# A Mamba and FFN block on one core: decays from a PSUM tile into a four-slot SBUF ring, and single-row loads of the B and C rows

## The reference

```python
def _L0_attn_ref(x, W_xproj, W_dt, b_dt, A_log, Dp):
    xz = jnp.einsum('btd,pd->btp', x, W_xproj)
    dt_raw = xz[..., :dt_rank]                     # dt_rank 64, d_s 16
    Bm = xz[..., dt_rank:dt_rank + d_s]
    Cm = xz[..., dt_rank + d_s:]
    dt = jax.nn.softplus(jnp.einsum('btr,dr->btd', dt_raw, W_dt) + b_dt)
    A = -jnp.exp(A_log)
    dA = jnp.exp(dt[..., None] * A)
    dBx = dt[..., None] * Bm[:, :, None, :] * x[..., None]
    def step(h, inp):
        dA_t, dBx_t, C_t = inp
        h = dA_t * h + dBx_t
        y = jnp.einsum('bds,bs->bd', h, C_t)
        return (h, y)
    ...
    return ys.transpose(1, 0, 2) + Dp * x

x = L0_attn_x                                      # (16, 1024, 256) float32
x = _layernorm(x + _L0_attn_ref(x, ...), axis=-1)
x = _layernorm(x + _L0_ffn_ref(x, w_gate, w_up, w_down), axis=-1)   # silu(gate) * up, hidden 768
```

## Time and profile before

| What | Before |
|---|---|
| Median of 3 runs | 2022.29 us (2020.32 to 2025.22) |
| The profiled execution's own time | 2022.87 us |
| Its span, first to last instruction | 2021.1 us |
| DVE busy | 1869.1 us, 92% of the span |
| POOL busy | 1768.4 us, 87% |
| PE busy | 1729.2 us, 86% |
| ACT busy | 1474.9 us, 73% |
| TensorE's mean granted clock | 0.947 |
| Transfers' share of 16 DMA engines | 33.3% |

### The profile page before, as it was taken

The page is one execution under the profiler, slowest core; times in us unless marked ns, Lnnn a source line. Parts: engine busy times, 40 slices in busy tenths (PEclk is TensorE's granted clock), DMA queues, the critical chain, the costliest instruction groups (busy, mean ns, idle before and its releaser), DMA issues.

```text
span 2021.1 us, 35597 instructions
## 1 busy us (share of the span) xinstructions
PE 1729.2 (86%) x10664; PEld 1339.9 (66%) x10664; DVE 1869.1 (92%) x2317; ACT 1474.9 (73%) x2668; POOL 1768.4 (87%) x811
## 2 busy tenths in 40 slices
PE   5688888888889888889888889888889888889887
PEld 3566676666677666777666776666766666766665
DVE  5899999999999999999999999999999999999993
ACT  6767777777777778777677877777777778776752
POOL 5998889988988988988988899989889989889970
PEclk7899999999999999999999999999999999999989
DMA  7234333233333233333234233234233243232300
GB/s 248 95 98 137 104 119 116 86 123 135 105 117 115 83 126 131 105 105 125 89 126 130 96 110 120 100 126 131 95 110 113 96 136 121 99 115 88 112 12 21
DMA packets 102675, 223.18 MB, mean 110 GB/s; under 512 B 9617, under 2 KB 44018, under 8 KB 102642
## 3 DMA queue, kind: packets, MB, share of 16 engines
q1 hardware_dynamic: 102642, 222.78, 33.3%
HBM read 203.87 MB, written 18.87 MB: 110 GB/s over the span
## 4 chain that ended last, share of the span: by engine, by line
PE 49%; issue 15%; ACT 14%; DVE 13%; POOL 7%; DVEq 1%; ACTq 0%; POOLq 0%; DMA 0%; SPq 0%
PE p_o L997 16%; PE p_y L960 13%; PE p_m L984 6%; POOL h L416 5%; DVE h L707 4%; DVE hid L743 3%; DVE h L699 3%; ACT p_da L533 3%; PE p_m L908 3%; PE p_c L937 3%; PE p_m L900 3%; ACT da_k L533 2%; ACT res_n L576 2%; PE p_da L928 2%; DVE silu_g L737 2%
## 5 line engine op out<-in xcount | busy, mean ns | idle before, releaser
L406 POOL TENSOR_TENSOR ub<-u,b_bc 128x1024 f32<-128x1024 f32 x384 | 906.1, 2375 | 0.1
L416 POOL TENSOR_TENSOR h<-h,c_bc 128x1024 f32<-128x1024 f32 x320 | 757.0, 2378 | 0.0
L533 ACT ACTIVATE p_da<-dt,neg_a 128x512 f32<-128x512 f32 x768 | 524.1, 686 | 231.2 <-DVE h L699 229.2
L960 PE MATMUL p_y<-ident,h 128*128 128x128 f32 x4096 | 566.2, 290 | 36.9 <-POOL h L416 36.7
L960 PEld LDWEIGHTS p_y<-ident,h 128*128 128x128 f32 x4096 | 509.7, 150 | 87.0 <-POOL h L416 52.0
L699 DVE TENSOR_TENSOR_SCAN h<-p_da,h_carry,ub 128x512 f32<-128x512 f32 x384 | 474.5, 1266 | 9.2 <-ACT p_da L533 8.3
L699 DVE TENSOR_TENSOR_SCAN h<-p_da,ub 128x512 f32<-128x512 f32 x384 | 452.4, 1208 | 15.0 <-ACT p_da L533 9.3
L997 PE MATMUL p_o<-wt_down,hid 128*128 128x256 f32 x1536 | 352.3, 379 | 3.0 <-DVE res L750 1.6
L997 PEld LDWEIGHTS p_o<-wt_down,hid 128*128 128x128 f32 x1536 | 284.4, 190 | 52.2 <-issue 14.7
L984 PE MATMUL p_m<-x_t,wt_up 128*128 128x512 f16 x744 | 194.3, 384 | 81.1 <-DVE hid L743 81.1
L707 DVE TENSOR_TENSOR h<-h,p_c 128x1024 f32<-128x1024 f32 x192 | 229.9, 1197 | 25.3 <-PE p_c L937 25.3
(11 more groups left out here) (101 smaller groups left out, 1875.7 us busy)
## 6 DMA issues: line engine op xcount, KB each, us to landing
b_bc<-bc_rows_dram SPq DMA_DIRECT2D x128, 768.0 KB, 4.0
c_bc<-bc_rows_dram SPq DMA_DIRECT2D x320, 256.0 KB, 4.2
x_in<-in_L_attn_x SPq DMA_DIRECT2D x32, 512.0 KB, 3.5
out_x<-res_n SPq DMA_DIRECT2D x32, 512.0 KB, 3.0
bc_rows_dram<-bc_rows SPq DMA_DIRECT2D x32, 64.0 KB, 1.6
hid<-in_L_ffn_w_gate SPq DMA_DIRECT2D x1, 768.0 KB, 4.9
hid<-in_L_ffn_w_up SPq DMA_DIRECT2D x1, 768.0 KB, 6.8
res<-in_L_ffn_w_down SPq DMA_DIRECT2D x1, 384.0 KB, 7.2
```

The source lines that it names most:

```text
L406: nc.gpsimd.tensor_tensor(ub[:, i % UB_SLOTS, :, :], u[:, par, :, :], b_bc[:, i:i + 1, :].broadcast_to([P, DH, T]), ALU.mult).then_inc(s_u ...
L416: nc.gpsimd.tensor_tensor(h[:, s % H_SLOTS, :, :], h[:, s % H_SLOTS, :, :], c_bc[:, i:i + 1, :].broadcast_to([P, DH, T]), ALU.mult).then_i ...
L533: nc.scalar.activation(da, dt[:, par, q, :], ACT.Exp, scale=neg_a[:, q, s:s + 1]).then_inc(s_da, 1)
L960: ins = nc.tensor.matmul(p_y_tok[:, k, q * P:(q + 1) * P], h[:, s % H_SLOTS, q, k * P:(k + 1) * P], ident[:, :], start=False, stop=(s == S ...
```

## The change

Four things change.

1. All decays go to one ring `da` in SBUF with four slots. ACT makes them three states ahead (`DA_AHEAD` 3), where it made them one ahead. `da_k` goes. The PSUM tile, renamed `p_ub`, holds the transposed inputs of the K states and nothing else, and PE fills it earlier.
2. The K states are 8, 11, 13 and 14 in place of 3, 7, 11 and 15, and their ACT product is made three states ahead in place of two. The ten states that POOL multiplies by C are 0, 1, 3, 4, 5, 6, 7, 11, 13, 14. `UB_AHEAD` falls from 4 to 3.
3. `b_bc` and `c_bc` become rings of six and five slots. Each row has a load of its own, so a chunk has 12 loads of B and ten of C in place of four and ten. The bytes stay the same.
4. The table `AT` has other numbers.

```diff
-POOL_STATES = (0, 1, 2, 3, 4, 7, 8, 9, 10, 11)
+POOL_STATES = (0, 1, 3, 4, 5, 6, 7, 11, 13, 14)
-UB_AHEAD = 4
-DA_AHEAD = 1
+UB_AHEAD = 3
+DA_AHEAD = 3
+DA_SLOTS = 4
-    "dt_of": (7, 1), "u_of": (7, 1),
+    "dt_of": (7, 0), "u_of": (10, 0),
-K_STATES = (3, 7, 11, 15)
-K_AHEAD = 2
+K_STATES = (8, 11, 13, 14)
+K_AHEAD = 3
-        da_k = sb("da_k", [P, K_SLOTS, DH, T], F32)
+        da = sb("da", [P, DA_SLOTS, DH, T], F32)
-        b_bc = sb("b_bc", [P, NB, T], F32)
-        c_bc = sb("c_bc", [P, NP, T], F32)
+        b_bc = sb("b_bc", [P, B_SLOTS, T], F32)
+        c_bc = sb("c_bc", [P, C_SLOTS, T], F32)
-        p_da = ps("p_da", [P, DH, T])
+        p_ub = ps("p_ub", [P, DH, T])
...
             def broadcast_b(c, j, par):
+                if j >= B_SLOTS:
+                    sp.wait_ge(s_ub, NB * c + (j - B_SLOTS + 1))
+                elif not (isinstance(c, int) and c == 0):
+                    wait(sp, s_ub, NB * (c - 1) + (j - B_SLOTS + NB + 1))
+                s = B_STATES[j]
+                sp.dma_start(b_bc[:, j % B_SLOTS:j % B_SLOTS + 1, :], bc_dram[par:par + 1, s:s + 1, :].broadcast_to(
+                    [P, 1, T])).then_inc(s_b[j % B_SLOTS], 16)
...
             def decay(c, s, par, q):
                 act.wait_ge(s_dt, c + 1)
-                if s in K_STATES:
...
-                    da = da_k[:, i % K_SLOTS, q, :]
-                else:
-                    wait(act, s_scan, 2 * units(c, s) - 2 + q - 1)
-                    da = p_da[:, q, :]
-                nc.scalar.activation(da, dt[:, par, q, :], ACT.Exp, scale=neg_a[:, q, s:s + 1]).then_inc(s_da, 1)
+                wait(act, s_scan, 2 * (units(c, s) - DA_SLOTS) - 1 + q)
+                nc.scalar.activation(da[:, s % DA_SLOTS, q, :], dt[:, par, q, :], ACT.Exp,
+                                     scale=neg_a[:, q, s:s + 1]).then_inc(s_da, 1)
...
                 if s in K_STATES:
                     wait(dve, s_ub_ps, DH * (k_units(c, s) - 1) + q + 1)
-                    da, dbx = da_k[:, K_STATES.index(s) % K_SLOTS, q, :], p_da[:, q, :]
+                    dbx = p_ub[:, q, :]
                 else:
                     i = B_STATES.index(s)
                     if q == 0:
                         dve.wait_ge(s_ub, NB * c + (i + 1))
-                    da, dbx = p_da[:, q, :], ub[:, i % UB_SLOTS, q, :]
+                    dbx = ub[:, i % UB_SLOTS, q, :]
...
-                nc.vector.tensor_tensor_scan(h[:, s % H_SLOTS, q, :], da, dbx, initial, ALU.mult, ALU.add).then_inc(s_scan, 1)
+                nc.vector.tensor_tensor_scan(h[:, s % H_SLOTS, q, :], da[:, s % DA_SLOTS, q, :], dbx, initial,
+                                             ALU.mult, ALU.add).then_inc(s_scan, 1)
...
             def ub_transposed(c, s, q):
                 i = K_STATES.index(s)
                 pe.wait_ge(s_ubt, TT * k_units(c, s))
-                wait(pe, s_scan, 2 * units(c, s) - 2 + q - 1)
+                if i > 0:
+                    wait(pe, s_scan, 2 * units(c, K_STATES[i - 1]) - 1 + q)
+                else:
+                    wait(pe, s_scan, 2 * units(c - 1, K_STATES[-1]) - 1 + q)
```

More of the change, by code:

```diff
@@ L35 @@
     "weights": (7, 1),
-    "x_transposed": (2, 1), "x_out": (2, 1), "project": (3, 0), "rank_out": (4, 1), "bc_out": (4, 1),
-    "project_dt": (4, 1), "softplus_abs": (5, 1), "softplus_exp": (6, 0), "softplus_log": (6, 1),
-    "dt_of": (7, 1), "u_of": (7, 1),
[3 rows of a table removed]
-    "gate_up": (9, 1), "tanh": (9, 0), "silu": (10, 0), "hidden": (10, 1),
[3 rows of a table removed]
-    "bc_turned": (7, 1), "bc_cols": (9, 1),
-}
-K_STATES = (3, 7, 11, 15)
-K_AHEAD = 2
+    "x_transposed": (0, 2), "x_out": (3, 0), "project": (3, 0), "rank_out": (4, 1), "bc_out": (4, 1),
+    "project_dt": (4, 0), "softplus_abs": (5, 1), "softplus_exp": (5, 1), "softplus_log": (6, 0),
+    "dt_of": (7, 0), "u_of": (10, 0),
[3 rows of a table added]
+    "gate_up": (9, 0), "tanh": (9, 0), "silu": (10, 0), "hidden": (10, 1),
[3 rows of a table added]
+    "bc_turned": (8, 0), "bc_cols": (11, 1),
+}
+K_STATES = (8, 11, 13, 14)
+K_AHEAD = 3
 K_SLOTS = 2
-GROUP = 4
 UB_SLOTS = 6
+B_SLOTS = 6
+C_SLOTS = 5
 H_SLOTS = 8
@@ L75, in mamba_ffn_block @@
     NB = N - NK
-    B_GROUP = NB // NK
-    assert K_STATES == tuple(range(GROUP - 1, N, GROUP)) and B_GROUP == GROUP - 1
-    assert NB % UB_SLOTS == N % H_SLOTS == NK % K_SLOTS == 0
+    assert NB % UB_SLOTS == N % H_SLOTS == NK % K_SLOTS == N % DA_SLOTS == 0
+    assert NB == 2 * B_SLOTS and NP == 2 * C_SLOTS and K_STATES[0] > 0
     sum_at = {s: s + SUM_LAG[s in POOL_STATES] for s in range(N)}
     SUM_ORDER = sorted(range(N), key=lambda s: (sum_at[s], s))
-    assert all(sum_at[s] < N or s not in POOL_STATES for s in range(N))
+    assert N - 1 not in POOL_STATES
     x_chunks = x.rearrange("b (h k p) d -> (b h) p k d", p=P, k=TT)
@@ L162, in mamba_ffn_block @@
         p_m = ps("p_m", [P, 2, T])
-        tail_ps = (p_m, p_da)
+        tail_ps = (p_m, p_ub)
         tail_t = (tanh_g[:, :], ub[:, 0, 0, :])
@@ L199, in mamba_ffn_block @@
         s_rows_dram = sem("s_rows_dram")
-        s_b = [sem(f"s_b{k}") for k in range(N // GROUP)]
+        s_rows_kept = sem("s_rows_kept")
+        s_b = [sem(f"s_b{j}") for j in range(B_SLOTS)]
         s_ut_ps = sem("s_ut_ps")
@@ L209, in mamba_ffn_block @@
         s_c_ps = sem("s_c_ps")
-        s_c = [sem(f"s_c{i}") for i in range(NP)]
+        s_c = [sem(f"s_c{i}") for i in range(C_SLOTS)]
         s_hc_dve = sem("s_hc_dve")
@@ L334, in rows_out @@
                 sp.wait_ge(s_rows_dram, 16 * (c + 1))
[L336 to L350, removed]
@@ L352, in _, with broadcast_b @@
-            rows_out(0, 0)
-            for k in range(N // GROUP):
-                broadcast_b(0, k, 0)
-                broadcast_c(0, k, 0)
-            def step(c, par, batch, nxt, core, prev, last):
[L358 to L361, removed]
+                sp.sem_inc(s_rows_kept, 1)
+            def broadcast_b(c, j, par):
+                if j >= B_SLOTS:
[5 more added lines that the diff above has]
+                    [P, 1, T])).then_inc(s_b[j % B_SLOTS], 16)
@@ new lines, in broadcast_c @@
+            def broadcast_c(c, i, par):
+                if i >= C_SLOTS:
+                    sp.wait_ge(s_hc_pool, NP * c + (i - C_SLOTS + 1))
+                elif not (isinstance(c, int) and c == 0):
+                    wait(sp, s_hc_pool, NP * (c - 1) + (i - C_SLOTS + NP + 1))
+                s = N + POOL_STATES[i]
+                sp.dma_start(c_bc[:, i % C_SLOTS:i % C_SLOTS + 1, :], bc_dram[par:par + 1, s:s + 1, :].broadcast_to(
+                    [P, 1, T])).then_inc(s_c[i % C_SLOTS], 16)
@@ new lines, in _ @@
+            rows_out(0, 0)
+            for i in range(C_SLOTS):
+                broadcast_b(0, i, 0)
+                broadcast_c(0, i, 0)
+            broadcast_b(0, 5, 0)
+            for j in range(6, 9):
+                broadcast_b(0, j, 0)
+            def step(c, par, batch, nxt, core, prev, last):
+                if core:
+                    broadcast_b(c, 9, par)
+                    broadcast_b(c, 10, par)
+                    broadcast_c(c, 5, par)
+                    broadcast_b(c, 11, par)
+                    broadcast_c(c, 6, par)
@@ L493, in bc_out @@
                 act.wait_ge(s_proj_ps, c + 1)
-                wait(act, s_rows_dram, 16 * c)
+                wait(act, s_rows_kept, c)
                 wait(act, s_ones, 3)
@@ L593, in _ @@
                 u_out(0, a)
+            for s in range(1, DA_AHEAD):
+                for q in range(DH):
+                    decay(0, s, 0, q)
             act.wait_ge(s_const, 1)
@@ L925, in ub_transposed @@
                 pe.wait_ge(s_ubt, TT * k_units(c, s))
-                wait(pe, s_scan, 2 * units(c, s) - 2 + q - 1)
+                if i > 0:
+                    wait(pe, s_scan, 2 * units(c, K_STATES[i - 1]) - 1 + q)
+                else:
+                    wait(pe, s_scan, 2 * units(c - 1, K_STATES[-1]) - 1 + q)
                 for k in range(TT):
-                    ins = nc.tensor.transpose(p_da[:, q, k * P:(k + 1) * P],
+                    ins = nc.tensor.transpose(p_ub[:, q, k * P:(k + 1) * P],
                                               ub_t[:, i % K_SLOTS, k, q * P:(q + 1) * P], ident[:, :])
@@ L1015, in step @@
                         due = due_at(s, zone)
-                        if zone == 0 and core and s in K_STATES:
-                            ub_transposed(c, s, 1)
+                        if zone == 0 and core and s + 1 in K_STATES:
+                            ub_transposed(c, s + 1, 0)
                         if zone == 0:
@@ L1043, in step @@
                         if zone == 2 and core and s + 1 in K_STATES:
[L1044 removed]
+                            ub_transposed(c, s + 1, 1)
                         if zone > 0:
```

33 lines of the change are left out of this document (21 added, 12 removed), and 12 rows, old and new, of the table AT.

## The result

The changed kernel takes **2833.68 us** (median of 4 runs, 2833.45 to 2836.22) against 2023.52 for the kernel before on the same chip: a ratio of 1.401, 95% interval 1.399 to 1.403. It is 40% slower.

What follows compares the result with a forecast made beforehand. DVE was taken as the bound, 95% busy in the main part. POOL's 1738.5, B-state scans' 926.9 and POOL's small 57.1 us in turn, plus 21.0 and 52.0 at the ends, gave 2797 us; eight in ten 2050 to 2960.

Steps and rivals of the forecast that it cites:

- Exclusion: B-state scans with two SBUF inputs and POOL's multiplies exclude each other for whole instructions: 2797 us, 2676 to 2957; 65 in 100.
- the rule of the Trainium skill: A DVE instruction's second SBUF input uses the read interface shared with GpSimd; who starts first holds it throughout: 2797 us.
- my lower bound of 2676: Neighbouring instructions overlap at their edges; if handoffs between scans and multiplies do too, 121 us come off 2797.
- the idle time of the path: Path idle in slot 11 and at the norm: up to 5 us a chunk, +160 us, 2957; the plain sum takes none.
- my own sign of being wrong in size: Prediction wrong in size if the path idles over 5 us a chunk or a waiting scan holds back POOL's queue.
- both engines over 90% busy: In the changed kernel's profile, DVE and POOL would both look over 90% busy while doing the same number of instructions.
- The decay ring's gain: Three states of lead end DVE's 18.9 us of decay waits and most of 16.5 for K inputs: at most -35.4 us.
- half of the tanh wait: ACT no longer waits for a scan ahead of tanh, so half of DVE's 33.3 us wait goes: -16.7 us.
- the rival of separate paths: DVE's two SBUF inputs and POOL don't collide; scans last 1.2 to 1.3 us: 1970 us, 1929 to 2018; 20 in 100.
- The other edits, at nothing: Single-row loads, new K states, POOL's shorter lead and the table AT cost nothing: hidden in slack or only moving work.
- Word sharing: DVE and POOL share the path word by word: 2110 us, up to 2400; multiplies 2.4 to 2.6 us; 13 in 100.
- Doesn't do what it says: POOL, with three states of lead, starves DVE of ub as much as ACT's lead gives: 2022 us; 2 in 100.

Runs made afterwards that it cites:

- first experiment: Changed kernel, but B-state scans take their second input from PSUM tile p_ub instead of ub, and PE's transposes wait for the scan before: 2035.8 us, ratio 1.007.
- the streams: No reference work: DVE and POOL run independent instructions in nine phases, alone and together; scans with two SBUF inputs beside multiplies: 12 multiplies take 38.67 us, 3.22 each.

## Why the prediction was right

**The forecast case came.** Exclusion was given 65 in 100 and 2797 us; the time is 2834, 1.3% above, in the case's own range. One input's place decides (first experiment), no other edit is needed for it (2790.6 with the ring alone), it is POOL's reading that collides (fills harm nothing), and the path is held for whole instructions (halved multiplies halve the longest wait of a scan with a carry, from 3.33 - 1.27 to 2.36 - 1.27 us; the streams alternate one for one). By the rule of the Trainium skill that the prediction names, from "SBUF — State Buffer", section "Who interferes with whom", the trace agrees: 3.25 us for a multiply that meets a scan, 2.34 for one that doesn't, and no meeting with fills or with an input in PSUM.

**The sum was near by two errors that cancel.** I charged each pair of scan and multiply 1.21 + 2.36 = 3.57 us. It is 3.22: a scan adds 0.92 to the 2.30 of a multiply, since each hands over before its recorded end. With these, 736 x 2.30 + 768 x 0.92 = 2399 us in place of 2665.4; plus 57.1, 21.0 and 52.0 it is 2529. That is under even my lower bound of 2676, which took 121 us off where 266 were due. The other error is the idle time of the path: 2831.7 - 2529 = 303 us by difference, 9.5 us a chunk, where I allowed up to 5 and took none. Added up from the start and end times of the trace it is more: from 26 us to the end of the last scan there are 397 us, 12 a chunk, in which neither a B-state scan nor a product of POOL runs, and the path is in use for the other 2360, where I had charged 2722.5. More than 5 us a chunk was my own sign of being wrong in size. That the total came out 1.3% off is luck; the mechanism isn't. The idle time comes from the in-order queues: POOL stands 276.1 us before `rstd`, for DVE's `neg_mean`, and 308.2 before its products with C, for scans and the carries behind them, while DVE at times does work that doesn't need the path.

**What bounds it.** I expected both engines over 90% busy. DVE is at 98%, POOL at 77%. A scan that meets a busy POOL waits for up to a whole multiply, 2.1 us, and a multiply only 0.92 us for a scan. So DVE, which was the bound, got 914.5 us of waiting and POOL 375 (2113.5 - 1738.5); DVE ran behind and POOL waited for it. Halving the multiplies moved the bound to POOL.

**The decay ring's gain.** DVE's waits for decays are gone, as predicted. That they, the K inputs and half of the tanh wait are worth 52 us is not borne out: the two kernels with the lead and no collision take 2021.9 and 2035.8 us, not the 1970 of the rival of separate paths. ACT stops at its next wait instead, and DVE waits 71.5 and 31.1 us for tanh, 33.3 before. But these two can't settle it. In both every scan reads `p_ub`, so PE fills it just one scan ahead, and DVE waits 17.0 and 24.6 us for it, where I had taken most of 16.5 off. Where `p_ub` was left to the K states and POOL only wrote, DVE waited 0.6 us for it and 0.8 for tanh, and the time was 1978; but POOL had less work there. What the whole lead gives beside a fully loaded POOL stays open.

**The other edits, at nothing.** With the ring they cost 43 us (2833.7 against 2790.6, where the ring had two slots and a lead of one), the table 29 of them (2833.7 against 2804.5). Without the ring, at a lead of one, they cost 237 us, of which the table is 174. I had named no cover for the table. The runs show that it needs one and that a lead of three is enough: with it and without stretched scans all of these edits together are 14 us above the kernel before (2035.8 against 2022.1). The transfers were hidden as argued: POOL waited 0.1 us before its products with B, though a row needs 4.1 us to land.

**The rivals.** Separate paths (20 in 100) fell with the scans of 2.4 us. Word sharing (13 in 100) fell: in the streams a multiply lasts 2.34 us or 3.25, with nothing between, and a scan waits for all of it. (Half of the way from its 2110 to 2797 would have been some 2450 us, not the 2400 that I gave as its end; nothing rests on it.) "Doesn't do what it says" fell too: DVE waited for `ub` once, 5.0 us, as before.

No complete version that I ran beats the kernel before. A longer lead without the collision would need places for the decays in PSUM beside `p_ub`; it wasn't tried.

## What to carry to other kernels

Before moving an operand from PSUM to SBUF to gain slots, count the SBUF tensors of the instruction that reads it: here a DVE instruction with two of them took turns with POOL's multiplies and copies, and a DVE copy from SBUF to SBUF did so with one. Price that as whole instructions in turn (a scan of 512 beside a multiply of 1024: 3.22 us for the pair), find who waits longer, and keep POOL's instructions short if it can't be avoided. A wait of an engine with slack, such as ACT's 229 us, is worth what the bound engine waits for it, and in the kernel with the lead and the old table even those 18.9 us came back as another wait.

## What the runs showed of the hardware

The alternation is strict. With both queues full, exactly one scan runs for each multiply, and each scan waits 2.1 us (3.22 - 1.12), although both engines had their next instruction ready all the time. What a turn adds to a multiply goes with the length of DVE's instruction and not with its columns: 0.92 us for a scan of 512, and 0.98 us for a product of 1024, where the first multiply found the path free, (38.41 - 2.34)/11 = 3.28 us. Undisturbed the two last nearly the same, 1.20 and 1.21 us. A POOL copy of 1024 columns, which reads one tensor, collides as well: the first lasts 1.04 us, the other eleven 1.96 to 1.97, and the scans beside them 1.98. So does a DVE copy from SBUF to SBUF, though it has a single input: (32.55 - 2.34)/11 = 2.75 us for a multiply, 0.45 more than alone, by a copy that lasts 0.68 us undisturbed. I had looked at instructions with two inputs only. The column of `h_carry` beside an SBUF input does not collide: such scans stay within 1252 to 1285 ns.
